# Window attention: scores with the keys on the partitions, maxima and mask added inside the products, heads written out through DRAM

## What is computed

```
q, k = rope(h @ Wq), rope(h @ Wk);  v = h @ Wv          (h: layer norm of X)
s[i, j] = q[i] . k[j] / 4
seen = (same 64-block | i < 4 | j < 4 | |i - j| <= 128) & (j <= i)
X += softmax(s where seen) @ v, heads joined, @ Wout
```

## Time and profile before

| | us |
|---|---|
| three timed executions | 3493.97, 3483.92, 3475.99 |
| their median | 3483.92 |
| profiled execution, device time | 3482.07 |
| its span, first to last instruction | 3480.1 |
| mean granted TensorE clock | 0.915 of 2.4 GHz |

### The profile page before, as it was taken

The page is one execution under the profiler, slowest core; times in us unless marked ns, Lnnn a source line. Parts: engine busy times, 40 slices in busy tenths (PEclk is TensorE's granted clock), DMA queues, the critical chain, the costliest instruction groups (busy, mean ns, idle before and its releaser), DMA issues. The chain is left out here.

```text
span 3480.1 us, 59852 instructions
## 1 busy us (share of the span) xinstructions
PE 2885.8 (83%) x18120; PEld 1810.9 (52%) x18120; DVE 2095.5 (60%) x4691; ACT 1684.5 (48%) x3357; POOL 961.4 (28%) x1635
## 2 busy tenths in 40 slices
PE   6599999999970999959836999778588888797869
PEld 3244444444340898845515899634355555544434
DVE  6578888887358444445485444356477777326852
ACT  4257777777710445411113544312466666254545
POOL 3322222222110445411013544334222222020112
PEclk9679999999985999979967999989899999898879
DMA  7722233233132443330032443312211111000001
GB/s 255 248 63 83 73 85 84 73 83 87 32 113 68 103 95 80 71 73 0 0 122 79 85 90 80 79 52 79 76 51 51 52 51 49 17 1 13 0 14 49
DMA packets 170495, 248.63 MB, mean 71 GB/s; under 512 B 29241, under 2 KB 113593, under 8 KB 170321
## 3 DMA queue, kind: packets, MB, share of 16 engines
q1 hardware_dynamic: 145744, 212.88, 19.6%
q0 software_dynamic: 24576, 33.57, 6.0%
HBM read 152.94 MB, written 92.27 MB: 70 GB/s over the span
## 5 line engine op out<-in xcount | busy, mean ns | idle before, releaser
L1919 DVE CUSTOM_DVE_ANT_0 s0Ah_SD<-s0Ah_ps_s,s0Ah_table 128x1024 f32<-128x1024 f32 x512 | 607.0, 1222 | 157.4 <-PE s0Ah_ps_s L1974 157.4
L1943 ACT ACTIVATE s0Ah_PM<-s0Ah_ps_x 128x512 f32<-128x512 f32 x1024 | 530.1, 602 | 188.2 <-PE s0Ah_ps_x L1999 98.1
L1974 PE MATMUL s0Ah_ps_s<-s0Ah_plus_k,s0Ah_plus_q 48*128 48x512 f32 x1024 | 422.9, 477 | 33.8 <-DMA s0Ah_minus_k<-s0Ah_ones 29.9
L1899 POOL TENSOR_TENSOR s0Ah_DG<-s0Ah_SD,s0Ah_mx 128x128 f32<-128x128 f32 x512 | 204.6, 400 | 555.4 <-DVE s0Ah_mx L1919 555.4
L2185 ACT ACTIVATE s4Ch_PM<-s4Ch_SD,s4Ch_nb 128x260 f32<-128x260 f32 (+2 forms) x512 | 254.2, 497 | 146.3 <-POOL s4Ch_nb L2128 133.1
L1974 PEld LDWEIGHTS s0Ah_ps_s<-s0Ah_plus_k,s0Ah_plus_q 48*128 48x128 f32 x1024 | 167.4, 193 | 281.4 <-DVE s0Ah_mx L1919 176.7
L2019 PE MATMUL s0Ah_ps_v<-s0Ah_PM,s0A_V 128*17 128x512 f32 x2048 | 272.0, 603 | 0.0
L2139 DVE CUSTOM_DVE_ANT_0 s4Ch_SD<-s4Ch_ps_s,s4Ch_table 128x260 f32<-128x260 f32 (+2 forms) x512 | 204.8, 407 | 78.9 <-PE s4Ch_ps_s L2230 62.7
L1999 PE MATMUL s0Ah_ps_x<-s0Ah_plus_q,s0Ah_plus_k 50*128 50x512 f32 (+3 forms) x640 | 237.8, 388 | 0.0
L2230 PE MATMUL s4Ch_ps_s<-s4Ch_ks,s4Ch_qs 96*128 96x256 bf16 (+2 forms) x896 | 142.5, 229 | 112.5 <-DVE s4Ch_mx L2139 58.2
L1999 PE MATMUL s0Ah_ps_x<-s0Ah_minus_q,s0Ah_minus_k 50*128 50x512 f32 (+3 forms) x640 | 218.7, 389 | 0.0
(11 more groups left out here) (416 smaller groups left out, 7176.8 us busy)
## 6 DMA issues: line engine op xcount, KB each, us to landing
s0A_parts<-s0Ap_sp_top SPq DMA_DIRECT2D x32, 512.0 KB, 5.5
s0A_parts<-s0Ap_sp_rest SPq DMA_DIRECT2D x32, 512.0 KB, 5.5
s1M_raw_w<-in_L_ffn_w SPq DMA_DIRECT2D x16, 1024.0 KB
s3M_raw_w<-in_L_ffn_w SPq DMA_DIRECT2D x16, 1024.0 KB
s4C_parts<-s4Cp_sp SPq DMA_DIRECT2D x48, 256.0 KB, 2.4
s0Ah_plus_q<-s0A_parts SPq DMA_DIRECT2D x64, 128.0 KB
s0Ah_plus_k<-s0A_parts SPq DMA_DIRECT2D x64, 128.0 KB
s0Ah_minus_q<-s0A_parts SPq DMA_DIRECT2D x64, 128.0 KB
```

The costliest lines, as they stand in the source:

```text
L1899: nc.gpsimd.tensor_tensor(DG[p % 3][:, r * TB + t, :], SD[i % NSD][:, t * P:(t + 1) * P], mx[p % 3][:, r * TB + t:r * TB + t + 1].to_broad ...
L1919: nc.vector.tensor_tensor_reduce(SD[i % NSD][:, :], ps_s[i % 2][:, :, :].rearrange("p a n -> p (a n)"), table[:, (TB - 1 - t) * P:(TB - 1 ...
L1943: nc.scalar.activation(PM[n % NPB][:, :], ps_x[u % NX][:, :], ACT.Exp).then_inc(e_ok, 1)
L1974: x = nc.tensor.matmul(ps_s[i % 2][:, half, :], q[at(r), t * P:(t + 1) * P], k[at(r), half * GT:(half + 1) * GT], start=True, stop=True)
```

## The change

- `heads_window` is written anew in the manner of `heads_decay`. First pass, queries on the partitions, 40 tiles ahead (`AHEAD = 2 * U + U // 2`): only for the maxima. The four global keys now stand ahead of every key block of 128 (`KBLK` = 132), so a tile's keys are one run of 264 (128 for the first tile). DVE adds the mask and takes the maximum as before, unscaled.
- Second pass, keys on the partitions. A PSUM bank holds two key blocks of one head. A product of the identity with a mask tile (`hide`, 0 or -1e30) opens it over all 512 columns; then two products of 99 rows (96 of the stack and three rows of maxima in BF16 parts against ones) add s - max. ACT takes the exponential of 512 (or 384) columns at once, scale 1/4 inside. The four global keys get their own products for queries from tile 2 on. No transposes of probabilities.
- Values: V (17 columns a head) against the probabilities in F32, four products side by side, in two bursts per pair, one pair behind.
- Maxima: turned by TensorE, negated by ACT, split in three by POOL, and written as rows by six DMAs a pair that POOL issues.
- Loads: nine a pair on SP into five buffers. Stores: five a pair; `OD` is laid out so that `project_heads` reads 64 rows in one run, and the sums have a tensor of their own, `OS`. Both attentions get that. `project_heads` replaces `project_out` in the window attention.
- `SplitBlocks` replaces `Split`: q and k parts of their own, k in blocks of 132 whose first four columns POOL fills from the sequence's first keys; q and k go through the split one after the other; DVE's order in a group is moments, products of q, residue of the group before, products of k, rows of the norm. All loops are written out.

The parts of the diff that the prediction speaks of:

```diff
+            def load(p):
+                s = p % NST
+                q, k, done = Q[s], K[s], st_in[s]
+                rows = slice(2 * p * HD, 2 * (p + 1) * HD)
+                both = lambda t: t.rearrange("(r d) t -> d r t", r=2)
+                sp.dma_start(q[0:3 * HD, :, :], qparts[rows, :, :].rearrange("(r d) n t -> (d n) r t", r=2)
+                             ).then_inc(done, 16)
+                sp.dma_start(q[5 * HD:6 * HD, :, :], both(qparts[rows, 0, :])).then_inc(done, 16)
+                sp.dma_start(k[5 * HD:6 * HD, :, :], both(kparts[rows, 2, :])).then_inc(done, 16)
+                for r in range(2):
+                    one = slice((2 * p + r) * HD, (2 * p + r + 1) * HD)
+                    sp.dma_start(k[0:3 * HD, r, :], kparts[one, 0:1, :].to_broadcast([HD, 3, TB * KBLK])
+                                 ).then_inc(done, 16)
+                    sp.dma_start(q[3 * HD:5 * HD, r, :], qparts[one, 0:2, :]).then_inc(done, 16)
+                    sp.dma_start(k[3 * HD:5 * HD, r, :], kparts[one, 1:2, :].to_broadcast([HD, 2, TB * KBLK])
+                                 ).then_inc(done, 16)
...
+            def maxima(p):
+                pool.wait_ge(e_ok, START + turn_use(p) + 1)
...
+                for n in range(PARTS):
+                    for r in range(2):
+                        pool.dma_start(Q[p % NST][96 + n:97 + n, r, :].rearrange("a (t q) -> a t q", t=TB),
+                                       NMp[p % 2][n][r * TB:(r + 1) * TB, :]).then_inc(rows_in[p % 2], 16)
...
+            def shifted(p, r, blk, n):
+                t = 2 * blk + n
...
+                x = nc.tensor.matmul(bank[:, 2 * n * P:2 * n * P + w],
+                                     k[0:99, r, t * KBLK + NGL:(t + 1) * KBLK], q[0:99, r, t * P:t * P + w],
+                                     start=False, stop=(n == 1))
...
+            for p in range(NP):
+                pe.wait_ge(rows_in[p % 2], ROWS * (p // 2 + 1))
+                for j in range(U):
+                    blk, r, n = j // 4, j % 2, j % 4 // 2
+                    if n == 0:
+                        hidden(p, r, blk)
+                    if p * U + j + AHEAD < N:
+                        score(p * U + j + AHEAD)
+                    shifted(p, r, blk, n)
+                    if j in (3, 7, 15):
+                        global_scores(p, (3, 7, 15).index(j))
+                    if j == 11 and p + LATE < NP:
+                        turned(p + LATE)
+                    if j == 5 and p:
+                        global_values(p - 1)
+                        for t in (0, 4, 1, 5):
+                            values(p - 1, t)
+                    if j == 9 and p:
+                        for t in (2, 6, 3, 7):
+                            values(p - 1, t)
```

In `heads_decay` and `project_heads`:

```diff
-                sp.dma_start(OD[p, :, :], OE[p % 2][:, :]).then_inc(out_to[p % 2], 16)
+                for j in range(4):
+                    sp.dma_start(OD[j // 2, j % 2, p, :, :], OE[p % 2][j * 32:j * 32 + HD, :]
+                                 ).then_inc(out_to[p % 2], 16)
+                sp.dma_start(OS[p, :, :], OE[p % 2][HD:P:32, :]
+                             ).then_inc(out_to[p % 2], 16)
...
-                        sp.dma_start(OT[r * 64:(r + 1) * 64, g, c, :], OD[n:n + 4, z:z + HD, :]
+                        sp.dma_start(OT[r * 64:(r + 1) * 64, g, c, :],
+                                     OD[r, half, n:n + 4, :, :].rearrange("n d q -> (n d) q")
```

More of the change, by code:

```diff
@@ L1680, in _ @@
             load_once(sp, weights, pairs)
-            with sp.Fori(0, B) as b:
-                for h in range(HB):
-                    split.sync(sp, b, h)
+            for g in range(NG):
+                split.sync(sp, g)
             split.all_written(sp)
@@ L1692, in _ @@
             ln.pool(pool, 1)
-            def turn(b, h, first, more):
-                g = b * HB + h
-                pool.wait_ge(split.third, START + g - 1)
+            for g in range(NG):
+                h = g % 2
+                if g < NG - 2:
+                    ln.pool(pool, g + 2)
                 for s in range(2):
+                    if g >= 2 and s == 0:
+                        pool.wait_ge(split.rest, START + 2 * (g - 1))
                     pool.wait_ge(ab_ok, START + (2 * g + s + 1) * DC)
@@ L1715, in _ @@
             ln.vector(dve, 1)
-            def turn(b, h, first, more):
-                g = b * HB + h
+            for g in range(NG):
+                h = g % 2
                 now = lambda t: t[:, h * GT:(h + 1) * GT]
+                if g < NG - 2:
+                    ln.vector_moments(dve, g + 2)
                 for s in range(2):
@@ L2161, in turn @@
-            def turn(pr, first, last):
-                for u in range(U):
-                    if not (last and u >= U - 2):
-                        most(pr * U + u + 2, (u + 2) % U)
-                    if u % 2 == 1 and not (u % TB == 1):
-                        copy(pr * (U // 2) + u // 2, u)
-                    if u % G == 0 and not (first and u < 2 * G):
-                        v = u // G - 2
-                        norm(pr * 2 + v // 2, v % 2, pr * UH + v)
-            most(0, 0)
-            most(1, 1)
@@ new lines, in _ @@
+            nc.scalar.copy(same[:, :], ident[:, :])
+            act.wait_ge(sign_mm, START + 1)
+            for n, order in enumerate(((0, 1, 0, 2), (0, 2, 0, 2))):
+                for k, m in enumerate(order):
+                    x = nc.scalar.activation(hide[:, n, k * P:(k + 1) * P], ps_x[NX - 1][:, m * P:(m + 1) * P],
+                                             ACT.Copy, scale=1e30)
+            x.then_inc(hide_ok, 1)
+            act.wait_ge(clear_ok, START + 2)
+            for p in range(LATE):
+                negated(p)
@@ new lines, in _ @@
+            pe.wait_ge(sign_ok, START + 1)
+            for m in range(3):
+                x = nc.tensor.transpose(ps_x[NX - 1][:, m * P:(m + 1) * P], signs[:, m, :], ident[:, :])
+            x.then_inc(sign_mm, 1)
+            for i in range(AHEAD):
+                score(i)
+                for p in range(LATE):
+                    if i == (p + 1) * U + 2:
+                        turned(p)
+            pe.wait_ge(ones_ok, START + NST)
+            pe.wait_ge(hide_ok, START + 1)
+            pe.wait_ge(vz_ok, START + 1)
```

662 lines of the change are left out of this document (312 added, 350 removed).

## The result

Over four runs of each the kernel after takes 3305.3 us (3303.3 to 3309.3), the kernel before 3485.2 (3476.0 to 3494.0): a ratio of 0.9485, 95% interval 0.947 to 0.950. The forecast was 3292, 13 us too low and inside its own range. The profiled execution took 3305.05 us, 177 less than the profiled 3482.1 of before; the sum had 192.

The account below looks back on a forecast made before the run. TensorE was to bound the new window heads at 9.3 us a pair. 3482.1 - 180 (heads) - 11 (projections) + 6 - 7 (outputs) = 3290, on the median 3292; own range 3272 to 3322, whole range 3252 to 3355.

Parts of the forecast that it names:

- What bounds the pair: Window heads: TensorE sets the pair at 9.3 us; VectorE 6.9, ScalarE at most 7.3, SP 7.9, POOL 7.5.
- Rival 1: Window heads: POOL's DMAs cost 1.36 us, chain of maxima 14.3, a pair 10.9, +51 us: 3343; chance 0.24.
- rival 4: Window heads: POOL's DMAs cost 2.4 us and land at 4.5, a pair 16.9, +243 us: 3535; chance 0.03.
- The +8 us: By the Trainium skill's later start of software-written descriptors, the maxima chain is about 12.5 us, the sum some 8 longer.
- TensorE's price, 9.3 us a pair: Window heads: 13,424 BF16 columns at 0.46 ns give 6.2 us, F32 values 3.0, with the transpose of maxima 9.3.
- The coupling: Window heads: bursts of values (2.0 and 1.0 us) against banks feeding DVE and ACT; given nothing beyond the 0.46's gaps.
- rival 3: Window heads: weight loads of 44 BF16 products stand in the open, +4.3 us a pair, +138: 3430; chance 0.06.
- rival 2: Window heads: TensorE without gaps at 8.6 us a pair and cheap DMAs, -22 and -4 us: 3266; chance 0.15.
- The chain of the maxima: Window heads: transpose to landed rows takes 12.1 us over 1.31 pairs, so a pair is at least 9.2; just hides at 9.3.
- Start and end: Window heads: first shifted product at 31 us; 1.6 us at the end for the last exponential and collection.
- Projections, -11: Second attention's projections: new order removes TensorE's 1.42 us wait for DVE's cosine products, 8 x 1.4; range -14 to +8.
- Outputs, -7 and +6: Attention outputs both near 51 us with loads at 0.46: first -7, second +6; if loads don't get faster, 0 and +13.

Follow-up runs that it names:

- three bursts: Window heads' value products in three bursts a pair instead of two, on the kernel after with full-size global-key weights, trimmed mask and two V tensors: 3279.9 us.
- proj: The kernel after with VectorE's and GpSimd's order in the projections put back to that of before: 3328.9 us, ratio 0.955.
- order: The kernel before with the new order alone in the second attention's projections, old layout and whole residues: 3474.3 us, ratio 0.9957.

## Why the prediction was nearly right

**What bounds the pair.** Right. TensorE is the bound, and most other prices were high: maxima 0.35 us apart against 0.43, ScalarE 6.2 us a pair (194 of 307 us) against 7.3, GpSimd 4.6 against 7.5 because a DMA is 0.5 and not 1.0. Only SP was priced a little low, 8.2 us (9.75 less its 1.5 of waits) against 7.9. None set the pair. Rival 1 fell with the price of a DMA, rival 4 with it. The Trainium skill ("DMA: Bandwidth & Descriptors", Latency and other measured facts) has such DMAs start later than SP's. The median landing here, 2.4 us, is below the 2.8 of SP's stores in the earlier trace rows, but those are larger and go to DRAM, and for the same rows issued by SP the profile has no landing; so no run here shows the delay or rules it out. The +8 us didn't come, because a chain of 8.4 us hides 0.4 more.

**TensorE's price, 9.3 us a pair: 0.45 too low.** This is the largest term that was mis-sized. The mean of 0.46 ns a column was taken over 13,424 columns. The products cost less by their columns (0.42 to 0.44, 5.8 us in all against 6.2), but 1,536 of these columns are in products with four-column weights, and those cost 0.19 us more than their columns, three times a pair: 0.57. Another 0.3 are gaps of under 0.1 us, mostly where BF16 products and values meet. The first attention, the model for the price, has no product with four-column weights. The run with full-size weights gives back 0.39 of the 0.45 us a pair, 8.9 us of the stage. So the total came within 13 us in part by luck: the pairs are 14.4 us over, the projections 3.6, and the start of the stage gave 7.7 back. The coupling, to which the text gave "nothing beyond the gaps in 0.46", doesn't show at 9.75 us; at 9.36 an order with shorter bursts gives 0.17 us a pair back.

**Weight loads in the open, rival 3.** Wrong for the full-size weights, as the forecast held: products of 256 columns with new 99-row weights come every 0.115 us, though each load takes 0.10. But its mechanism is there in small, at the four-column weights, where two loads stand in the open each time. Part 3 of the Trainium skill's "TensorE: Matmul & The Clock Gate", by which full-height loads don't overlap, is contradicted by this trace as by the earlier trace rows, as far as full-size weights follow each other. **Gapless TensorE, rival 2**, at 8.6: no; even the best order has 9.19.

**The chain of the maxima.** Right that it hides, by more than "just": 8.4 us against 12.1. But the room was read too wide as well. From step 11 to the next pair are five steps of 16 and yet only 1.83 us (2603.55 to 2605.38), as the bursts of values lie in the other eleven; the chain has 1.19 pairs and not 1.31. Six more DMAs showed where it ends, and that GpSimd's pauses, which the prediction didn't have, are part of it.

**Start and end.** The start took 23.3 us, not 31: first product 8.8 us in instead of 11.9, the maxima 6.2 for 7.7, the chain 8.3 for 11 (the memsets on GpSimd, 12.6 us in all, end before it, as was said). The end took 5.7 us, not 1.6, for the last pair's values come after its exponentials with nothing beside them. 23.3 + 32 x 9.75 - 5.2 + 5.7 = 335.8; start and end are off by -7.7 and +4.1, the pairs by +14.4.

**Projections, -11.** The order gave -8.1, the layout beside it +0.4. The failed step is the count "8 x 1.4": TensorE's wait for VectorE stands in five groups of eight, 6.5 us in all, which the view of waits of the whole stage has in one row, and I multiplied one group's row. What the other 1.6 us of the order's 8.1 come from is open. The step "132-wide blocks cost nothing while PE is the bound" was right in its sum and blind in its reason: the wait they bring to ScalarE costs up to 14 us, and it is the new order that covers it. For the case that "that cover goes" the prediction had 8 x 1 us; it is nearer 14.

**Outputs, -7 and +6.** Measured -6.5 and +7.2. Loads are 0.60 us, not 0.46, and that costs nothing: TensorE has its first rows and then runs through.

**What beats both.** The kernel of the three bursts: 3279.9 us, ratio to before 0.9417 (0.940 to 0.944) against 0.9485 (0.947 to 0.950) of the change.

## What to carry to other kernels

Price a matmul by its columns only while the weights keep their shape; look for the odd product, here with weights four columns wide among full ones, see in the weight loads' rows whether its load still runs beside the product before, and fill it up if its rows are free. Where an engine is the bound with few buffers around it, order counts beyond the sum: here shorter bursts gave some 9 us of the stage, and work moved to an engine with over a third of its time free lost 5. And test an order and a layout apart: here the order alone is worth -8 us, the layout alone +15, both together -8.

## What the runs showed of the hardware

A DMA of 2 KB issued by GpSimd took it 0.50 us and landed 2.4 us later (median of 192). GpSimd pauses in the middle of such DMAs for 2.3 to 2.9 us: once in the kernel after with its 192, three times 120 apart with 384 of them, four times 126 apart with 576; what it does there no view shows. A BF16 product with 4-column weights between full ones cost 0.19 us more than one with 128 columns of weights, since its load (0.08 us) and the next one (0.10 us) didn't run beside a product. VectorE's residue of K took 3.38 us in most groups of the kernel after, 1.22 in its last one and throughout proj: in the timeline it is slow beside GpSimd's 3.2 us sum, at the same moment, which is slower too (2.45 alone). Where they don't meet both are fast. One of the pairs: the sum runs from 2324.83 to 2328.03, the residue from 2325.74 to 2329.12, and so ends 1.1 us after the sum, about what it takes alone. So it looks as if it stood still until the sum was done; no run tests it. It cost little, since neither was the bound: the stage is 0.4 us longer than in the run order, where the whole residue takes 2.28 us.
